# Last layer of a four-layer kernel: two tiles' high parts ahead of the low ones, the router's products two later, input scales first

## What is computed

```
def _L3_ffn_ref(x, weight, bias, gate_w, in_channel_scale, out_channel_scale):
    xf = x.reshape(-1, H)
    router_logits = xf @ gate_w.T
    routing = jax.nn.softmax(router_logits.astype(jnp.float32), axis=1).astype(x.dtype)
    in_scale = routing @ in_channel_scale
    out_scale = routing @ out_channel_scale
    wb = ste_sign(weight)
    out = xf * in_scale @ wb.T * out_scale + bias
    return out.reshape(B, S, -1)
...
    x = x + _L3_ffn_ref(_L3_cond_ref(x, cond_128, ...), ...)
```

## Time and profile before

| | us |
|---|---|
| median of three runs | 545.47 |
| lowest, highest | 545.13, 546.2 |
| the profiled execution's own time | 545.86 |
| its span, first to last instruction | 544.0 |
| first scale product of the last layer, from the span's start | 486.94 |
| PE busy | 531.5 (98% of the span) |
| DVE, ACT, POOL busy | 243.2, 140.9, 157.5 |

### The profile page before, as it was taken

The page is one execution under the profiler, slowest core; times in us unless marked ns, Lnnn a source line. Parts: engine busy times, 40 slices in busy tenths (PEclk is TensorE's granted clock), DMA queues, the critical chain, the costliest instruction groups (busy, mean ns, idle before and its releaser), DMA issues.

```text
span 544.0 us, 6969 instructions
## 1 busy us (share of the span) xinstructions
PE 531.5 (98%) x2647; PEld 394.1 (72%) x2647; DVE 243.2 (45%) x537; ACT 140.9 (26%) x247; POOL 157.5 (29%) x153
## 2 busy tenths in 40 slices
PE   7999999999999999999999999999999999989996
PEld 6788888888888888888888886636455445577774
DVE  3543242732323722223622224544525258897775
ACT  5322222322222322222322222000002217545232
POOL 3599992310000400000300930040002000127666
PEclk9999999999999999999999999999999999999999
DMA  8498440197000140000205000959796919589763
GB/s 287 143 421 308 138 102 0 39 153 137 0 0 0 58 116 0 0 0 0 84 13 130 8 1 0 151 129 165 192 197 174 227 39 218 105 153 209 181 136 117
DMA packets 82502, 61.60 MB, mean 113 GB/s; under 512 B 61744, under 2 KB 66864, under 8 KB 81712
## 3 DMA queue, kind: packets, MB, share of 16 engines
q1 hardware_dynamic: 77696, 41.83, 35.0%
q0 software_dynamic: 4704, 19.40, 14.2%
q10 hardware_dynamic: 80, 0.08, 0.0%
HBM read 38.98 MB, written 12.81 MB: 95 GB/s over the span
## 4 chain that ended last, share of the span: by engine, by line
PE 92%; DVE 5%; issue 1%; ACT 1%; DMA 1%; POOL 0%; DVEq 0%; POOLq 0%
PE ps L659 89%; DVE cT L1171 1%; DVE xs L1171 1%; PE ps L849 1%; DVE c_lo L1171 1%; DMA pack_a<-in_pack_a 1%; DVE cT L1345 0%; DVE c_lo_odd L1171 0%; PE ps L810 0%; DVE t L1171 0%; PE ps L966 0%; PE ps L863 0%; ACT c_hi L1045 0%; ACT c_hi_odd L1045 0%; ACT wT L1045 0%
## 5 line engine op out<-in xcount | busy, mean ns | idle before, releaser
L659 PE MATMUL ps<-c_lo,wl 128*128 128x512 f32 x448 | 173.0, 390 | 0.3 <-POOL c_lo L514 0.3
L659 PE MATMUL ps<-c_hi,wl 128*128 128x512 f32 x448 | 173.0, 390 | 0.1
L1171 DVE TENSOR_TENSOR hff<-silu,ps 128x512 f32<-128x512 f32 x56 | 38.5, 687 | 163.5 <-PE ps L659 163.5
L659 PEld LDWEIGHTS ps<-c_lo,wl 128*128 128x128 f32 x448 | 84.1, 188 | 18.7 <-POOL c_lo L514 0.7
L659 PEld LDWEIGHTS ps<-c_hi,wl 128*128 128x128 f32 x448 | 84.0, 188 | 18.0 <-ACT c_hi L1045 0.8
L659 PE MATMUL ps<-wl,h_hi 128*128 128x512 f32 x224 | 87.7, 391 | 0.0
L659 PE MATMUL ps<-wl,h_lo 128*128 128x512 f32 x224 | 87.2, 389 | 0.0
L1045 ACT ACTIVATE h_hi<-hff 128x512 fp32r<-128x512 f32 x56 | 35.4, 632 | 112.5 <-DVE hff L1171 112.5
L1079 ACT ACTIVATE silu<-ps 128x512 f32<-128x512 f32 x56 | 33.5, 598 | 116.4 <-PE ps L659 116.4
L1171 DVE TENSOR_TENSOR h_lo<-hff,h_hi 128x512 fp32r<-128x512 f32 x56 | 45.9, 820 | 39.1 <-ACT h_hi L1045 39.1
L659 PE MATMUL ps<-wbase,cT 128*128 128x512 f32 x128 | 56.5, 594 | 0.0
(11 more groups left out here) (181 smaller groups left out, 581.8 us busy)
## 6 DMA issues: line engine op xcount, KB each, us to landing
wl<-in_wl POOLq DMA_DIRECT2D x14, 768.0 KB, 9.4
stg<-y_dram SPq DMA_DIRECT2D x64, 128.0 KB, 5.1
xs<-in_x SPq DMA_DIRECT2D x4, 1024.0 KB, 7.9
x_all<-in_x SPq DMA_DIRECT2D x1, 4096.0 KB, 14.7
y_dram<-prod SPq DMA_DIRECT2D x16, 256.0 KB, 2.2
x_dram<-x_all SPq DMA_DIRECT2D x4, 1024.0 KB, 6.9
x_all<-cS POOLq DMA_DIRECT2D x4, 1024.0 KB, 7.6
x_all<-in_bias POOLq DMA_DIRECT2D x4, 1024.0 KB, 10.4
```

The source lines that it names most:

```text
L659: return pe.matmul(o, l, r, start=start, stop=stop)
L1171: return dve.tensor_tensor(o, a, b, op)
```

## The change

The number of products and of all other operations stays the same; what moves stands in the queues of PE, ACT and DVE; POOL and SP are as before.

- PE, group 0: in_scales stands ahead of out_scales(0); the fourth out_scales product and router3(1) stand behind tile 0's lows; the high parts of tiles 0 and 1 stand together ahead of the lows of tile 0, and tile 1's lows behind the router.
- PE, groups 1 and 2: router3(g + 1) stands two products later, behind tile 1's first chunk. turn_logits3 keeps its four products behind the router. turn_routing stands behind tile 2 as a whole, so that four products, not six, stand between it and in_scales. (In group 0 too there are now four.)
- PE, group 3: its first out_scales product stands right behind in_scales(3); the highs of tiles 0 and 1 together, as in group 0.
- ACT, group 3: osc of tile 0 is copied behind the first high part, not the second.
- DVE, group 0: the fourth chunk of cond3(1) is stored behind the low parts.

```
+            def high_products(g, j):
+
+                pe.wait_ge(s_osc, GT * g + j + 1)
+                for s in range(S):
+                    pe.wait_ge(s_scaled_hi, S * g + s + 1)
+                    mm(bank(j), halves(g)[0][:, s, cols(j)], sgn[:, s], s == 0, False)
+
+            def low_products(g, j):
+
+                for s in range(S):
+                    pe.wait_ge(s_scaled_lo_odd if s % 2 else s_scaled_lo_even, 2 * g + s // 2 + 1)
+                    ins = mm(bank(j), halves(g)[1][:, s, cols(j)], sgn[:, s], False, s == S - 1)
+                ins.then_inc(s_product[3], 1)
...
-            out_scales(0, (0,))
             in_scales(0)
-            out_scales(0, (1, 2, 3))
-            pe.wait_ge(s_scaled, 1)
-            router3(1)
+            out_scales(0, (0, 1, 2))
             for g in range(G - 1):
-                sign_product(g, 0)
-                if g:
-                    router3(g + 1)
-                sign_product(g, 1, (0, 1))
-                turn_logits3(g + 1)
-                sign_product(g, 1, (2, 3))
-                sign_product(g, 2, (0, 1, 2))
-                turn_routing(g + 1)
-                sign_product(g, 2, (3,))
-                sign_product(g, 3, (0, 1))
-                in_scales(g + 1)
-                sign_product(g, 3, (2, 3))
-                out_scales(g + 1, (0, 1, 2))
+                if g == 0:
+                    high_products(0, 0)
+                    high_products(0, 1)
+                    low_products(0, 0)
+                    out_scales(0, (3,))
+                    router3(1)
+                    low_products(0, 1)
+                    turn_logits3(1)
+                    sign_product(0, 2)
+                    sign_product(0, 3, (0,))
+                    turn_routing(1)
+                    sign_product(0, 3, (1, 2))
+                    in_scales(1)
+                    sign_product(0, 3, (3,))
+                else:
+                    sign_product(g, 0)
+                    sign_product(g, 1, (0,))
                     router3(g + 1)
+                    sign_product(g, 1, (1, 2))
+                    turn_logits3(g + 1)
+                    sign_product(g, 1, (3,))
+                    sign_product(g, 2)
+                    turn_routing(g + 1)
+                    sign_product(g, 3, (0, 1))
+                    in_scales(g + 1)
+                    if g + 2 == G:
+                        out_scales(g + 1, (0,))
+                    sign_product(g, 3, (2, 3))
                 if g + 2 < G:
+                    out_scales(g + 1, (0, 1, 2))
                     cond3(g + 2, lambda: out_scales(g + 1, (3,)))
                 else:
-                    sign_product(g + 1, 0)
-                    out_scales(g + 1, (3,))
-            for j in range(1, GT - 1):
+                    out_scales(g + 1, (1, 2))
+            high_products(G - 1, 0)
+            high_products(G - 1, 1)
+            low_products(G - 1, 0)
+            out_scales(G - 1, (3,))
+            low_products(G - 1, 1)
+            for j in range(2, GT - 1):
                 sign_product(G - 1, j)
...
                 high(0)
+                if g == G - 1:
+                    out_scale(0)
                 high(1)
-                if g > 0:
+                if 0 < g < G - 1:
                     out_scale(0)
...
                 if g == 0:
-                    cond3(1, [(s, s) for s in range(S)])
+                    cond3(1, [(s, s) for s in range(S - 1)])
...
+                if g == 0:
+                    cond3(1, [(S - 1, S - 1)], S - 1)
```

More of the change, by code:

```diff
@@ L1382, in final2, with cond3 @@
                                              ALU.add).then_inc(s_x_new[2], 1)
-            def cond3(g, chunks):
+            def cond3(g, chunks, first=0):
                 dve.wait_ge(*bias_ready(3, g))
-                for n, (s, b) in enumerate(chunks):
+                for n, (s, b) in enumerate(chunks, first):
                     dve.wait_ge(s_cond_mm[3], S * g + n + 1)
```

## The result

The change makes the kernel slower, not faster. Over 13 runs of each the median went from 545.47 to 546.65 us; the ratio is 1.0026 with a 95% interval of 1.0016 to 1.0037, that is +1.4 us (+0.9 to +2.0; the medians themselves lie 1.2 apart), where 545.2 had been forecast. The profiled execution took 546.86 us (span 545.0) against 545.86 (544.0). Its parts, measured from PE's first scale product of the last layer (486.94 before, 486.97 now), are these. Where the number of products between two marks has changed, 0.23 us a product is allowed for.

What follows compares the result with a forecast made beforehand. PE was taken to bound the kernel (92% of the chain that ended last), so only its idle time counted; 1.1 + 0.15 - 0.8 - 0.76 = -0.3 us took the median from 545.47 to 545.2, range 544.1 to 546.2.

Steps and rivals of the forecast that it cites:

- First opening, +1.1: Group 0 of the last layer, to the first logits: a loss of +1.1 us, bounds +0.1 and +1.3.
- Steps (a) to (d): First opening: PE starts at 486.88, DVE scales from 487.38, ACT's osc at 488.31, then highs; tile 0's lows end at 493.50.
- One aside of the forecast: First opening: without turns with POOL, DVE's lows would end 2.50 behind 489.96, and the opening cost about +0.9.
- Routers, -0.40 each: Groups 1 and 2: two products now ahead of the router cover its wait for stored chunks; -0.8 us in all.
- in_scales, +0.05 each: Input scales, three times: four products instead of six cover ACT's copy of wT; +0.15 us in all.
- Rival 2: The wait moves from router to in_scales, where PE waits for wT three times, 0.40 each: 546.2 us, chance 0.12.
- Last opening, -0.76: Group 3: tile 2 begins 0.76 us sooner relative to in_scales, the lows being there in time; bounds -0.55 and -0.91.
- It counts at full speed: PE's clock shows 9 in all 40 slices, so any term changing PE's row of work counts at full speed.
- Rival 1: Both openings: the lows, not ACT, set the pace; sum -1.6, 543.9 us, chance 0.18.
- rival 3: Both openings: ACT keeps 0.61 us per high part; sum +0.1, 545.6 us, chance 0.15.
- The slower outcome: Whole kernel slower than 546.56 us: chance 0.05, from a third of rival 2 and tails.

Runs made afterwards that it cites:

- POOL variant: The whole change, with POOL's second low part in group 3 waiting for the fourth high part instead of the third, no operation added: ratio 0.9999, median 545.24 against 545.32.
- DVE variant: The kernel before, with DVE's first low part in group 3 waiting for the fourth high part, no operation added: ratio 1.0038, median 547.4.

## Why the prediction was wrong

The median, 546.65, lies 0.45 us above the range and on the other side of no change. The forecast's own narrower range was added up too tightly: its terms' bounds sum to -1.6 and +0.5, 543.8 to 546.0, not 544.6 to 545.7; the result lies outside that too. By the steps:

**First opening, +1.1, right.** It was 1.3 in the profiled run and 1.2 by the run of that part alone. Steps (a) to (d) held within 0.2: PE's first high came at 489.65 (reckoned 489.45), osc of tile 0 at 488.39 (reckoned 488.31), fourth high's product and tile 1's bank as the gate, first low at 492.65 (492.58), DVE's lows ending at 493.10 (493.04), 0.55 behind POOL's. The router ended at 495.19 (495.09). The rest is a slower row of tile 1's lows, 1.04 instead of 0.93, since its first product follows the router. The cause named (the router left a gap) was shown by putting it back. One aside of the forecast was misread: the 2.50 of DVE's two lows before already holds POOL's turns (in the last opening two took 2.38 around a POOL low of about 1.28, which leaves about 0.55 for each), so it is no price for lows that wait for nobody.

**Routers, -0.40 each, and in_scales, +0.05 each: right.** Together -0.36 and -0.31 in the trace, and -0.5 (medians) to -0.7 us (ratio) for both in their own run. Rival 2 did not come: in_scales follows turn_routing by 1.43, without a wait.

**Last opening, -0.76: the step that failed, in one clause.** "The lows are there (POOL 533.65, DVE 534.20 against a need at 534.51)" carried over the old times of DVE and POOL. The forecast had priced the two engines' turns in the first opening, but never asked in the last one whose turn came first. Its own rows gave the answer: POOL's second low waits for the third high part, which starts at 531.16 in the old order and at 531.11 in the forecast's. With DVE's first low at 531.82 and POOL's second at 531.86, 0.05 less turns DVE's lead of 0.04 into a tie. In the runs, ACT's osc now stands where ACT waited for DVE's second chunk, the third high part comes earlier, POOL's low starts 3.41 behind in_scales(3) instead of 3.47 and DVE's 3.45 instead of 3.43. POOL came first, and DVE lost two turns, not one: DVE's lows ended 6.93 behind in_scales(3) instead of 5.81. That makes all but 0.01 of the 0.99 us between forecast and measurement in this opening: PE's last low started 0.87 later than in a row, and the product behind it 0.11 later still. Both directions were shown, by the POOL variant (the loss goes) and the DVE variant of the kernel before (it appears). The Trainium skill, in "SBUF — State Buffer" ("Who interferes with whom"), says that issue order decides which of the two blocks and that an operation with two inputs in SBUF on DVE blocks against a GpSimd one that reads SBUF. The traces agree: DVE's two lows took 3.48 to 3.50 where POOL came first in the new order and 2.38 where DVE did.

This one step is enough for the miss: with the last opening as forecast, 546.65 would have been 545.7, inside the range.

**PE's clock: a term that was not in the sum.** "It counts at full speed" was read from 40 nines of the kernel before. The forecast itself added 0.8 us of idle time in the first opening, and there, in the trace of a lowered run, the granted clock falls to 0.50. The lowered mean clock stands in 11 of 25 runs of the whole change, and costs 1.25 us by the trace and 1.6 to 1.9 by the runs' medians. At full clock the change costs +1.0 by the trace and +0.6 to +0.9 by the medians; five lowered runs in 13 add about 0.6, which makes the +1.4 measured. No rival carried it. By itself it would have left the forecast inside its range. What decides between the two heaps of runs is open: full-clock and lowered runs have the same program, and the first group's part alone met it once in 12.

**Rivals.** Rival 1 (lows pace both openings) is out by the highs' times; rival 3 (ACT at 0.61 a high) too, since ACT's four highs took 2.18 with distances of 0.53. The slower outcome had 0.05, for a mechanism that did not come.

## What to carry to other kernels

Work that is moved behind something that waits should first be asked what gap it was filling: the router, where it stood, did not delay the first low, and where it was put it cost 1.2 us. Where two engines take turns at one resource, list their starts side by side around the change; if they lie within a tenth of each other, price both orders, and if one order is wanted, make it certain by the queue's order (here one line of DVE's, ahead of a step that nobody waits for). Idle time that is added on PE can cost more than itself if the clock falls behind it.

## What the runs showed of the hardware

- Two operations, one on DVE and one on POOL, each reading two tensors in SBUF, take turns by whole operations: the listed duration of the one that comes second grows by the rest of the first (POOL 1.79 against 1.28, DVE 3.48 in two against 2.38). The listed starts do not tell the winner at 0.04 us: in the run with the tiny DVE operation DVE was listed later and still went first.
- After an idle gap of 0.8 us and products that came one by one, PE's granted clock fell from 1.00 to 0.50 (2.4 to 1.2 GHz) in the first opening of one trace of the whole change and one of the POOL variant; the mean clock was lowered in 11 of 25 and 2 of 11 of their runs. In the trace of the DVE variant it fell in the tail, behind waits of 0.66 and 0.95; four of its five runs were lowered. A wait of 0.72 in the last opening (that part alone, 11 runs) and highs one by one without the gap ahead (router put back, 17 runs) lowered none.
- A new tensor of 32 bytes a partition, put ahead of other ones, went with a first layer whose long row of products was 2.7% slower (327.2 against 318.6 us); one of 256 bytes did not. That it is the operands' position is inferred; no run varied it alone.
